# Attention in a four-layer graph network: destination rows gathered into their own tiles and added on GpSimd

## The chip, the cores and the metric

The kernel runs on one core of one Trainium2 chip. Times are microseconds (us) on the device for one execution; a change is judged by the median of several runs. The names of the engines are those of the profile: PE is TensorE's matmul, PEld its weight load, DVE is VectorE, ACT is ScalarE, POOL is GpSimd, SP is SyncE, which here only issues DMAs.

## The reference, cut to what matters

Four graph layers run one after another over 6,250 nodes with 160 features (64 scalars and 32 vectors of 3) and 100,000 edges sorted by destination. Each adds its result to x. The change lies in layer 2, an attention layer. What its edges begin with is, for every edge, the sum of two rows that were computed per node:

```
s_src, v_src = node rows mapped by Ws_src, Wv_src      # table[2]
s_dst, v_dst = node rows mapped by Ws_dst, Wv_dst      # table[3]
message[e]   = row_src[src[e]] + row_dst[dst[e]]       # 160 floats for each edge
```

The sum is weighted by a map of the edge attributes, multiplied with the edge's 4 numbers (scalar and vector products), mapped, gated and multiplied once more; that gives the edge's scores and its value row. A softmax over the edges of each destination and a weighted sum follow in later passes.

## The kernel before

Edges are padded and cut into NG = 196 groups of 512: TG = 4 tiles of P = 128 edges, one edge to a partition. `attention_pass` is the stage that the change touches. It holds one program for each engine, every one a loop over the groups (`steps`, with an unroll of U = 4), joined by semaphores alone. `at_least` is a wait; `gate` is several waits, the first on a semaphore that has long been settled.

- SP's step i loads `ends[s]` for group i (the 4 columns of source indices and the 4 of destination indices, s = i mod 4), once `joined[s]` says that the slot's old indices have been used. Behind that, in the same queue, come the edge attributes of group i-2, the scores of group i-4 and the message rows of group i-7.
- POOL's step i waits for the indices of group i and for `made1` of group i-4 (the DVE has finished its first part on the group that held the tile `g[s]`; K1 = 13 operations), and issues four gathers from table[2] (L1114), one for each 128 x 160 tile of `g[s]`. Then it waits until group i-1's four gathers have landed (`fetched`) and issues four gathers from table[3] into the same tiles with `compute_op=ALU.add` (L1121). They count `joined`.
- ACT waits for `joined` in `scale_rows` and writes `gy` (L1216), four operations for a group. Its other work takes PE's transposes and maps out of PSUM (L1226, L1252) and applies the gates (L1265, L1267).
- DVE runs, for each group, `first` (group i: reads `g`, waits for `joined`), `message` (group i-3) and `second` (group i-1). All of them are tensor_tensor operations recorded at L1304, 28 for a group. Those on `att_vy`, `att_p` and `att_dot`, the product with `att_gate` and the two sums that end `second` take both inputs from SBUF; the others have one in PSUM.
- PE transposes the features, and maps them with the value, attention and gate weights: 90 matmuls for a group.

POOL can be three groups ahead of the DVE at most, since there are FETCH = 4 slots of `g`. Nothing else runs on POOL in this stage.

Of the kernel before, what the change touches and what calls it, by code (L numbers as in the profile page):

```python
# [22 lines left out]
P = 128  # L23
# [21 lines left out]
def build(nc, A, out):  # L45
# [86 lines left out]
    with whole:  # L132
# [825 lines left out]
        def attention_pass():  # L958
# [12 lines left out]
            with ExitStack() as ctx:  # L971
# [15 lines left out]
                ea = pair("ea", [2 * QUARTER, 2 * P])  # L987
                y_all = sums_T[:, 0:NG * TG * YC]
                g = pair("g", [P, TG, FEAT], n=FETCH)
                gy = pair("gy", [P, TG, FEAT])  # L990
                at = NG * TG * YC

# [23 lines left out]
                ea_loaded = [sem(ctx, f"att_ea_loaded{s}") for s in range(2)]  # L1016
                y_loaded = sem(ctx, "att_y_loaded")
                fetched = [sem(ctx, f"att_fetched{s}") for s in range(FETCH)]
                joined = [sem(ctx, f"att_joined{s}") for s in range(FETCH)]
                scaled = sem(ctx, "att_scaled")  # L1020
                y0_done = sem(ctx, "att_y0_done")
# [19 lines left out]
                with nc.Block() as block:  # L1041

                    @block.sync
                    def _(sp):
# [31 lines left out]
                        def step(i, s, r):  # L1076

                            if live(i, NG):
                                at_least(sp, joined[s], 16 * TG * r)
                                sp.dma_start(ends[s][:, 0:TG], A["src_groups"][ds(i * P, P), :]).then_inc(ends_loaded[s], 16)  # L1080
                                sp.dma_start(ends[s][:, TG:2 * TG], A["dst_groups"][ds(i * P, P), :]).then_inc(ends_loaded[s], 16)
                            k = i - 2
# [23 lines left out]
                    @block.gpsimd  # L1106
                    def _(pool):
                        def step(i, s, r):
                            if live(i, NG):
                                gate(pool, (w_loaded, 16 * N_LOAD),  # L1110
                                     (ends_loaded[s], 32 * (r + 1)),
                                     (made1, (i - 3) * K1))
                                for t in range(TG):
                                    pool.indirect_dma_start(g[s][:, t, :], None, table[2],  # L1114
                                                            bass.IndirectOffsetOnAxis(ends[s][:, t:t + 1], 0)).then_inc(fetched[s], 16)
                            if live(i - 1, NG):
                                s1, r1 = back(s, r, 1, U)
                                gate(pool, (w_loaded, 16 * N_LOAD),
                                     (fetched[s1], 16 * TG * (r1 + 1)))
                                for t in range(TG):  # L1120
                                    pool.indirect_dma_start(g[s1][:, t, :], None, table[3],  # L1121
                                                            bass.IndirectOffsetOnAxis(ends[s1][:, TG + t:TG + t + 1], 0),
                                                            compute_op=ALU.add).then_inc(joined[s1], 16)

                        steps(pool, NG, 1, step, warm=8, unroll=U)

# [83 lines left out]
                    def _(act):  # L1210
                        def scale_rows(i, s, r):
                            gate(act, (w_made, 9),
                                 (made1, (i - 1) * K1),
                                 (joined[s], 16 * TG * (r + 1)))
                            for t in range(TG):
                                ins = nc.scalar.activation(gy[s % 2][:, t, :], g[s][:, t, :], ACT.Copy, scale=y0_of(i, t))  # L1216
                            ins.then_inc(scaled, 1)
# [60 lines left out]
                    def _(dve):  # L1278
# [34 lines left out]
                        def first(i, s, r):  # L1313
# [3 lines left out]
                            sca0, vec0 = gy[s % 2][:, :, 0:SC], gy[s % 2][:, :, SC:FEAT].rearrange("p t (c u) -> p t c u", c=XYZ)  # L1317
                            at_least(dve, made1, k)
                            at_least(dve, made2, (i - 1) * K2)
                            at_least(dve, joined[s], 16 * TG * (r + 1))  # L1320
                            tt(vy[:, :, :, :], vec, xyz(yy, 1, 4, VC), ALU.mult, made1)
                            cross_parts(vec, yy, made1)
                            dve.wait_ge(made1, k + 1)
# [495 lines left out]
```

## Time and profile before

| | |
|---|---|
| median of 3 runs | 9227.61 us (9198.25 to 9258.36) |
| span of the profiled execution | 7226.5 us |
| the median less that span | 2001.1 us |
| busy in the span | PE 6569.0 us (91%), PEld 5175.8 (72%), DVE 4888.2 (68%), ACT 3087.1 (43%), POOL 4427.4 (61%) |
| POOL instructions of the attention stage | 784 gathers at L1114, 784 at L1121, from 2723.3 to 5285.2 us |
| mean granted TensorE clock | 0.872 of full speed |

The profile's own execution has no separate time; its span runs from the first to the last instruction. What lies around the span is taken as the median less the span, and as the same for both kernels. The attention stage lies in the 16th to the 30th of the 40 slices.

### The profile page before, as it was taken

Reading aid. Unit: us, or ns where it says so; the run is one execution under the profiler, and the core shown is the slowest. Engines: PE = TensorE matmul, PEld = TensorE weight load, DVE = VectorE, ACT = ScalarE, POOL = GpSimd, SP = SyncE. Lnnn points to the kernel's source line nnn. Section 1 sums busy time; section 2 is a strip of 40 time slices with the busy share of each in tenths; the row PEclk is TensorE's granted clock in tenths of the full one; section 3 lists DMA queues with packets and bytes.
Section 4 is the critical chain, followed back from the end, with each engine's and each line's share of the span. In section 5 each row is a group of like instructions: output and inputs, shape, how many; then the busy total and the mean of one; then the engine's idle time right before and its main releaser. Section 6 shows DMA issues by size and latency. Waiting matters only on the chain. (4 is left out here: it accounts for less than half of the span.)

```text
span 7226.5 us, 182541 instructions
## 1 busy us (share of the span) xinstructions
PE 6569.0 (91%) x51671; PEld 5175.8 (72%) x51671; DVE 4888.2 (68%) x14416; ACT 3087.1 (43%) x8581; POOL 4427.4 (61%) x3934
## 2 busy tenths in 40 slices
PE   6999999799999857999999999999947879999998
PEld 3777778576666736878878777787836744777777
DVE  4666665476666545777777777777657975666665
ACT  2444443333333344666666666666530012333332
POOL 1777773277777216888877887878720011777772
PEclk9999997599999756889898888989778955999996
DMA  1222221222222213444444444444426701222221
GB/s 61 68 68 68 68 68 34 58 68 68 69 69 68 44 60 61 83 82 83 82 81 80 82 81 81 82 80 83 78 52 174 200 5 36 69 69 69 69 69 44
DMA packets 730807, 526.10 MB, mean 73 GB/s; under 512 B 244683, under 2 KB 677819, under 8 KB 730083
## 3 DMA queue, kind: packets, MB, share of 16 engines
q0 software_dynamic: 263424, 321.38, 22.1%
q1 hardware_dynamic: 467300, 203.73, 11.0%
q8 instruction: 39, 0.64, 0.0%
q14 instruction: 44, 0.36, 0.0%
HBM read 429.13 MB, written 95.55 MB: 73 GB/s over the span
## 5 line engine op out<-in xcount | busy, mean ns | idle before, releaser
L606 POOL DMA_INDIRECT l_edge_g<-node_table,l_edge_idx x2352 | 2281.7, 970 | 1124.3 <-issue 702.9
L649 PEld LDWEIGHTS l_edge_win_ps<-l_edge_hot,l_edge_prod 128*32 128x32 f32 (+2 forms) x23520 | 1515.3, 128 | 247.7 <-issue 170.4
L649 PE MATMUL l_edge_win_ps<-l_edge_hot,l_edge_prod 128*32 128x40 f32 (+2 forms) x23520 | 1620.9, 227 | 4.3 <-DVE sums_T L732 4.3
L1121 POOL DMA_INDIRECT att_g<-node_table,att_ends x784 | 1250.4, 1595 | 238.9 <-issue 238.6
L672 ACT ACTIVATE l_edge_gy<-l_edge_g,y 128x160 f32<-128x160 f32 x2352 | 811.7, 416 | 791.9 <-DMA l_edge_g<-node_table,l_edge_idx 789.3
L1114 POOL DMA_INDIRECT att_g<-node_table,att_ends x784 | 792.8, 1011 | 415.2 <-issue 281.3
L636 PE MATMUL l_edge_w_ps<-l_edge_wo,l_edge_h 128*128 128x384 f32 (+1 forms) x3136 | 907.1, 423 | 0.2 <-ACT l_edge_h L664 0.2
L664 ACT ACTIVATE l_edge_h<-l_edge_h_ps 128x256 f32<-128x256 f32 (+1 forms) x784 | 337.8, 431 | 1126.3 <-PE l_edge_h_ps L624 1076.6
L1141 PE MATMUL att_turn<-ident,sums_T 128*128 128x128 f32 (+1 forms) x4704 | 775.0, 309 | 30.1 <-ACT sums_T L1226 23.7
L636 PEld LDWEIGHTS l_edge_w_ps<-l_edge_wo,l_edge_h 128*128 128x128 f32 (+1 forms) x3136 | 536.8, 191 | 336.1 <-issue 171.7
L1226 ACT ACTIVATE sums_T<-att_turn 128x512 f32<-128x512 f32 (+1 forms) x1176 | 665.3, 591 | 216.7 <-PE att_turn L1141 211.8
L1141 PEld LDWEIGHTS att_turn<-ident,sums_T 128*128 128x128 f32 (+1 forms) x4704 | 572.6, 154 | 205.1 <-issue 119.0
L624 PE MATMUL l_edge_h_ps<-l_edge_ea,l_edge_wi 16*128 16x256 f32 (+1 forms) x1176 | 494.6, 500 | 81.2 <-ACT l_edge_h L664 27.7
L701 DVE TENSOR_TENSOR l_edge_vy<-l_edge_g,y 128x384 f32<-128x384 f32 x588 | 325.9, 554 | 255.5 <-DMA l_edge_g<-node_table,l_edge_idx 254.1
L708 DVE TENSOR_TENSOR l_edge_prod<-l_edge_w_ps,l_edge_g 128x256 f32<-128x256 f32 x588 | 247.9, 422 | 312.7 <-PE l_edge_w_ps L636 312.5
L1216 ACT ACTIVATE att_gy<-att_g,y 128x160 f32<-128x160 f32 x784 | 270.3, 416 | 272.2 <-DMA att_g<-node_table,att_ends 271.7
L703 DVE TENSOR_TENSOR l_edge_hot<-l_edge_hot,y 128x480 f32<-128x480 f32 x588 | 383.2, 652 | 0.0
L1198 PEld LDWEIGHTS att_o<-att_w_o1v,sums_T 128*128 128x128 f32 x1568 | 290.2, 218 | 108.4 <-issue 90.9
L697 DVE TENSOR_TENSOR l_edge_hot<-iota_win,dst_rel 128x160 f32<-128x160 f32 x588 | 192.4, 327 | 253.0 <-PE l_edge_win_ps L649 231.8
L1304 DVE TENSOR_TENSOR att_vec<-att_o,sums_T 128x384 f32<-128x384 f32 x196 | 109.3, 558 | 363.8 <-ACT att_gate L1267 357.3
L1181 PE MATMUL att_o<-att_w_o2s,sums_T 96*128 96x64 f32 x1568 | 334.7, 298 | 10.6 <-ACT sums_T L1226 1.5
L1199 PE MATMUL att_o<-att_w_o1v,sums_T 128*128 128x64 f32 x1568 | 341.3, 304 | 0.0
(232 smaller groups left out, 11533.8 us busy)
## 6 DMA issues: line engine op xcount, KB each, us to landing
l_messages<-att_rows SPq DMA_DIRECT2D x196, 320.0 KB
sum_msg<-l_messages SPq DMA_DIRECT2D x196, 320.0 KB, 3.6
l_edge_g<-node_table,l_edge_idx POOLq DMA_INDIRECT x2352
att_g<-node_table,att_ends POOLq DMA_INDIRECT x1568
node_table<-l_rows SPq DMA_DIRECT2D x245, 80.0 KB, 1.6
att_ea<-in_edge_attr_T SPq DMA_DIRECT2D x196, 64.0 KB
l_scores<-att_score SPq DMA_DIRECT2D x784, 2.0 KB
l_edge_idx<-in_src_groups SPq DMA_DIRECT2D x588, 2.0 KB, 1.7
```

What stands on the lines that cost most here:

```text
L606: pool.indirect_dma_start(g[s][:, t, :], None, rows_of, bass.IndirectOffsetOnAxis(idx[s][:, t:t + 1], 0)).then_inc(fetched[s], 16)
L624: nc.tensor.matmul(h_ps[0][0:HALVES * hid, 0:HC], wi[:, :], ea[s0][:, :]).then_inc(hidden[0], 1)
L636: ins = nc.tensor.matmul(w_ps[s2][:, n * HALVES:(n + 1) * HALVES, 0:wn], h[last][s2][:, n * P:(n + 1) * P], wo[:, :])
L649: ins = nc.tensor.matmul(at, q[:, t, lo:lo + width], to[:, t, kinds, :], start=t == 0, stop=t == TG - 1)
L664: nc.scalar.activation(h[n][s1][:, :], h_ps[n][0:HALVES * hid, 0:HC], act_fn, scale=scales[n]).then_inc(active[n], 1)
L672: ins = nc.scalar.activation(gy[sk % 2][:, t, :], g[sk][:, t, :], ACT.Copy, scale=y4[:, ds((k * TG + t) * 4, 1)])
L703: nc.vector.tensor_tensor(to[:, :, 1:1 + XYZ, :], to[:, :, 0, :].unsqueeze(2).to_broadcast([P, TG, XYZ, EDGE_WIN]), xyz.to_broadcast([P, T ...
L1114: pool.indirect_dma_start(g[s][:, t, :], None, table[2], bass.IndirectOffsetOnAxis(ends[s][:, t:t + 1], 0)).then_inc(fetched[s], 16)
L1121: pool.indirect_dma_start(g[s1][:, t, :], None, table[3], bass.IndirectOffsetOnAxis(ends[s1][:, TG + t:TG + t + 1], 0), compute_op=ALU.add ...
L1141: ins = nc.tensor.transpose(turn[bank][0:width, t * P:(t + 1) * P], f[:, t, at:at + width], ident[:, :])
L1199: ins = nc.tensor.matmul(o1[:, t, PV + VC:O1W], feat_T[0][:, 2, e], w_o1v[1][:, :])
L1226: nc.scalar.activation(feat_T[n][0:width, part, :], turn[bank][0:width, :], ACT.Copy).then_inc(count, 1)
```

## The change

The destination rows get tiles of their own, `g_dst[s]`, of the same size as `g[s]` (4 x 128 x 160 floats, four slots, 10,240 more bytes for each partition), and semaphores of their own, `fetched_dst[s]`. POOL's step i now issues eight plain gathers for group i. Then it waits for both sets of group i-1 and adds them in one GpSimd tensor_tensor of 128 x 640 floats. `joined` counts 1 for a group, from that add, where it counted 16 for each of four DMAs; the three waits on it (SP, ACT, DVE) are rewritten to match.

```
+                g_dst = pair("g_dst", [P, TG, FEAT], n=FETCH)
...
+                fetched_dst = [sem(ctx, f"att_fetched_dst{s}") for s in range(FETCH)]
...
                             if live(i, NG):
-                                at_least(sp, joined[s], 16 * TG * r)
+                                at_least(sp, joined[s], r)
...
                                 for t in range(TG):
                                     pool.indirect_dma_start(g[s][:, t, :], None, table[2],
                                                             bass.IndirectOffsetOnAxis(ends[s][:, t:t + 1], 0)).then_inc(fetched[s], 16)
+                                for t in range(TG):
+                                    pool.indirect_dma_start(g_dst[s][:, t, :], None, table[3],
+                                                            bass.IndirectOffsetOnAxis(ends[s][:, TG + t:TG + t + 1], 0)).then_inc(fetched_dst[s], 16)
                             if live(i - 1, NG):
                                 s1, r1 = back(s, r, 1, U)
                                 gate(pool, (w_loaded, 16 * N_LOAD),
-                                     (fetched[s1], 16 * TG * (r1 + 1)))
-                                for t in range(TG):
-                                    pool.indirect_dma_start(g[s1][:, t, :], None, table[3],
-                                                            bass.IndirectOffsetOnAxis(ends[s1][:, TG + t:TG + t + 1], 0),
-                                                            compute_op=ALU.add).then_inc(joined[s1], 16)
+                                     (fetched[s1], 16 * TG * (r1 + 1)),
+                                     (fetched_dst[s1], 16 * TG * (r1 + 1)))
+                                nc.gpsimd.tensor_tensor(g[s1][:, :, :], g[s1][:, :, :], g_dst[s1][:, :, :], ALU.add).then_inc(joined[s1], 1)
...
-                                 (joined[s], 16 * TG * (r + 1)))
+                                 (joined[s], r + 1))
...
-                            at_least(dve, joined[s], 16 * TG * (r + 1))
+                            at_least(dve, joined[s], r + 1)
```

## Rows read from the trace of the kernel before

**Rows 1.** The page's 40 slices of the span, in tenths.

```profile
PE   6999999799999857999999999999947879999998
...
POOL 1777773277777216888877887878720011777772
PEclk9999997599999756889898888989778955999996
```

**Rows 2.** Busy time in one stretch of the attention stage; (x) counts instructions.

```profile
2850.00:5250.00 2400.00, 2284.18 (x16554) 1905.90 (x16552) 1792.34 (x5151) 1521.05 (x4232) 1920.08 (x1474) 0.87 0.43 81
```

**Rows 3.** POOL's groups of instructions, 2850 to 5250: busy us, mean ns | idle before.

```profile
L1121 POOL DMA_INDIRECT att_g<-node_table,att_ends x738 | 1177.2, 1595 | 224.9 <-issue 224.9
L1114 POOL DMA_INDIRECT att_g<-node_table,att_ends x736 | 744.7, 1012 | 255.3 <-issue 255.3
```

**Rows 4.** POOL in order of time: start, us, instruction [idle before].

```profile
3997.09 1.76 POOL L1121 DMA_INDIRECT att_g<-node_table,att_ends  x1 [0.31 <-issue]
3999.15 1.02 POOL L1114 DMA_INDIRECT att_g<-node_table,att_ends  x1 [0.30 <-issue]
...
4011.71 1.01 POOL L1114 DMA_INDIRECT att_g<-node_table,att_ends  x1 [0.30 <-issue]
...
4478.17 1.04 POOL L1114 DMA_INDIRECT att_g<-node_table,att_ends  x1 [4.30 <-issue]
...
4492.23 1.41 POOL L1114 DMA_INDIRECT att_g<-node_table,att_ends  x1 [1.80 <-issue]
```

**Rows 5.** Who waited for whom, 2850 to 5250: us, times, longest.

```profile
ACT att_gy L1216 <- DMA att_g<-node_table,att_ends: 217.9, 85, 4.0
...
DVE att_vy L1304 <- DMA att_g<-node_table,att_ends: 185.3, 87, 3.3
...
PE att_turn L1195 <- ACT sums_T L1226: 81.6, 68, 2.1
```

**Rows 6.** The DVE in order of time, around one arrival of rows.

```profile
4001.27 0.56 DVE L1304 TENSOR_TENSOR att_vy<-att_g,sums_T 128x384 f32<-128x384 f32 x1 [1.77 <-DMA att_g<-node_table,att_ends]
```

**Rows 7.** Stretches of 10 us: PE, PEld, DVE, ACT, POOL busy, PEclk, DMA.

```profile
3980.00:3990.00 10.00, 8.37 (x74) 6.95 (x73) 6.32 (x19) 5.38 (x17) 8.12 (x6) 1.00 0.52 90
4200.00:4210.00 10.00, 10.00 (x48) 8.09 (x46) 2.10 (x6) 4.64 (x14) 7.87 (x8) 0.50 0.31 52
...
4250.00:4260.00 10.00, 9.76 (x83) 8.02 (x82) 8.82 (x27) 7.40 (x21) 8.08 (x6) 1.00 0.41 71
```

**Rows 8.** The DVE in order of time over one group, while rows lay ready.

```profile
4244.73 0.56 DVE L1304 TENSOR_TENSOR att_vec<-att_o,sums_T 128x384 f32<-128x384 f32 x1 [1.08 <-ACT att_gate L1267]
...
4245.91 0.56 DVE L1304 TENSOR_TENSOR att_vec<-att_vec,att_gate 128x384 f32<-128x384 f32 x1
...
4249.30 0.56 DVE L1304 TENSOR_TENSOR att_vy<-att_g,sums_T 128x384 f32<-128x384 f32 x1 [0.16 <-DVE sums_T L1304]
...
4250.88 0.28 DVE L1304 TENSOR_TENSOR att_dot<-att_vy 128x128 f32<-128x128 f32 x1
...
4255.81 0.56 DVE L1304 TENSOR_TENSOR att_vec<-att_o,sums_T 128x384 f32<-128x384 f32 x1 [1.00 <-ACT att_gate L1267]
```

**Rows 9.** POOL's groups of the whole span, shapes kept apart.

```profile
L182 POOL IOTA iota_i<- 128x64 int32 x1 | 0.2, 178 | 0.4 <-ACTq L168 0.4
```

**Rows 10.** POOL in order of time, in the node pass ahead of attention.

```profile
2572.97 16.68 POOL L330 TENSOR_TENSOR x<-x,sums_T 128x7840 f32<-128x7840 f32 x1 [25.50 <-ACT sums_T L318]
```

**Rows 11.** The DVE in order of time, in the same stretch.

```profile
2575.50 0.26 DVE L293 BATCH_NORM_STATS2 l_stat<-sums_T  x1
2575.79 13.96 DVE L270 TENSOR_TENSOR l_stat_part<-l_stat 128x49 f32<-128x49 f32 x1
2589.78 0.24 DVE L271 TENSOR_TENSOR l_stat_part<-l_stat 128x49 f32<-128x49 f32 x1
```

**Rows 12.** The DVE's groups with both inputs in SBUF, 2850 to 5250: first and last of 12.

```profile
L1304 DVE TENSOR_TENSOR att_p<-att_g,sums_T 128x256 f32<-128x256 f32 x368 | 154.1, 419 | 0.0
...
L1304 DVE TENSOR_TENSOR att_dot<-att_dot,att_vy 128x128 f32<-128x128 f32 x184 | 52.2, 284 | 0.0
```

## The prediction

> **What bounds the kernel now.** First the page's slices [rows 1]. The attention stage is the 16th to the 30th slice. In all but its first and last PE stands at 9 tenths and POOL at 7 or 8, with the granted clock at 7 to 9 tenths. Elsewhere POOL does other work that the change doesn't touch, so all of the effect lies in these 2,562 us.
>
> Next the windows and the groups by line, in a stretch without start or end [rows 2, 3]. 738 accumulating gathers are 184.5 groups, so a group takes 2400 / 184.5 = 13.01 us. POOL's share of it: 4 x 1.012 for the plain gathers, 4 x 1.595 for the accumulating ones, together 10.43 us. Ahead of each instruction POOL is idle for 0.30 us even when nothing holds it, as its timeline shows [rows 4]; the mean ahead of the accumulating ones is 224.9 / 738 = 0.305 us. With 8 x 0.305 = 2.44 us a group costs POOL 12.87 us. Only 0.14 us of the 13.01 is left. So POOL, counted as 80% busy, has hardly a free moment: it is either generating descriptors or in the fixed gap. What is left lies in a few places like the 4.30 and 1.80 us of [rows 4]; over the whole stage there are twelve such gaps (six pairs), 46 us in all.
>
> Then the waits: who feels POOL? ACT and DVE wait for the rows in about half of the groups, 217.9 and 185.3 us [rows 5]. PE hardly waits, though: 81.6 us on ACT. To see why, compare stretches of 10 us [rows 7]. With rows in hand and at full clock PE issues 83 matmuls in 10 us and is 98% busy; a group has 90 (16554 / 184), so it wants 10.8 us, and the DVE's timeline of one such group gives 4255.81 - 4244.73 = 11.1 us [rows 8]. That is faster than POOL's 12.87, so the rows run out and PE falls to 84% (3980 to 3990). Behind that the granted clock falls to 0.5, and PE does 48 matmuls in 10 us (a group in 19 us) while being 100% busy; POOL gets ahead by one to three groups, the clock comes back, and the stock is eaten again. Over the stretch the clock was 0.87. So POOL sets the pace of the mean, and PE's slow spells are mostly paid from time in which it would have waited for POOL. It is close, however: 11.1 / 0.87 = 12.8 us is what the other engines could do at this clock.
>
> **The change part by part.** *Gathers.* Four accumulating gathers go (1.595 us each), four plain ones come. The plain ones beside the same work took 1.012 us [rows 3]: 4 x 0.583 = 2.33 us less for a group. That it is the accumulation that costs the difference is taken from the two groups of rows, which differ in nothing else but the table and the index column.
>
> *The add.* One new instruction, 128 x 640 floats. The nearest row is POOL's own tensor_tensor on 128 x 7840 floats, 16.68 us, 2.13 ns per element of a partition [rows 10]; 640 of them are 1.36 us. A fixed part can't be told from one size; POOL's shortest iota took 0.18 us for 64 elements [rows 9], so I add 0.1 us. Then the gap of 0.305. The lower bound is 1.36 + 0.30 = 1.67 us.
>
> The upper bound comes from the DVE. While POOL added its 128 x 7840 elements, DVE statistics with one input went on, 0.26 us each, but the first DVE operation with two inputs from SBUF, 128 x 49 elements, took 13.96 us and ended 0.1 us after POOL's; the next one of the same size took 0.24 us [rows 10, 11]. So the two engines exclude each other for whole instructions when both read like this. In attention the DVE spends 1208 us of 2400 in such operations (twelve groups, [rows 12]), 50% of the time or 6.6 us for a group. An add that comes at a random moment finds one running every second time and waits half of its 0.3 to 0.56 us: 0.1 us in the mean. I take this because POOL should get in between two of them; the other end is that it gets in only when a run of them ends, which is the slower rival below. The trace has no row of a POOL add that comes second.
>
> The Trainium skill speaks against the change here: "SBUF — State Buffer", section "Who interferes with whom", says that a DVE instruction with two SBUF inputs and a GpSimd instruction that reads SBUF share one read interface, the later one blocking until the first ends. By that rule the trace agrees (13.96 us). By it the DVE would lose up to one add, 1.4 us, in a group as well, which the first sum below leaves out.
>
> *Sum on POOL.* 8 x 1.012 + 8 x 0.305 + 1.36 + 0.1 + 0.1 + 0.305 = 12.40 us for a group against 12.87: 0.47 us less, times 196 = 92 us.
>
> *Waits.* The add's gate now also names `fetched_dst` of group i-1. These gathers were issued before group i's eight, 10 us earlier; the last accumulating gather before a start of the DVE ended at 3998.85 and the DVE began at 4001.27, so a landing takes some 2.4 us [rows 4, 6]. The gate costs nothing. Behind it on POOL stand the next group's gathers. `joined` now comes from the add and without the 2.4 us of landing, which shifts the DVE and ACT but no rate. On SP the wait for `joined` stands ahead of the index loads; it asks for a group that was added over two groups ago, and is early. The stock is still three groups at most. Sixteen gathers and one add now lie ahead of the first rows (16 x 1.25 + 1.7 = 21.7 us) where eight plain and four accumulating ones and a landing did (10 + 7.4 + 2.4 = 19.8): +2 us once. At the end there is a stock, so nothing.
>
> *The DVE's loss.* When the rows are short, the DVE is idle before each add ends (it waited 1.77 us in [rows 6]), so the exclusion costs nothing there. When there is a stock, the DVE has 1.0 us of idle in its group of 11.1 [rows 8]; an add of 1.4 us inside its chain makes it 11.1 to 11.5 us, still under 12.4. I put it at nothing in the forecast. Its cover is the time that POOL keeps the others waiting; where that is gone, it costs up to 0.4 us for a group.
>
> *Sum.* 92 - 2 = 90 us less; the 46 us of held gaps stay. The profiled execution: 7226.5 - 90 = 7136.5 us of span, with 2001.1 around it 9137.6, say 9138.
>
> **The rivals.** *The clock holds the others (gain lost).* The change takes from the waits of PE 0.47 us for a group, but PE's slow spells were paid from these. If the clock stays at 0.87 and the DVE's loss counts, the others need 11.1 / 0.87 = 12.8 to 11.5 / 0.87 = 13.2 us for a group against 13.01: from 41 us less to 37 more, 9187 to 9265, middle 9225. For it: the granted clock was 0.87 in the mean of the stretch [rows 2], and the other engines are already this near. Against: the fall of the clock followed a stretch with PE at 84%, and stretches at 98% kept it; with POOL at 12.4, PE would be at 11.1 / 12.4 = 90%, and stay full for longer.
>
> *The add waits for a whole run of the DVE (slower).* The DVE's operations follow one another within 0.1 us, and from 4245.91 to 4251.16 nearly all have two SBUF inputs, a run of 5.25 us in 11.1 [rows 8]. If POOL gets in only at its end, a random arrival waits 5.25^2 / (2 x 11.1) = 1.24 us in the mean, in place of 0.1: 12.40 + 1.14 = 13.54 us, plus 0.14 as now, 0.67 us more than 13.01, 131 us: 9359. It turns the sign where the mean wait passes 0.1 + 0.47 = 0.57 us.
>
> *The clock rises.* If PE at 90% keeps its clock, the held gaps go (46 us), and with an add of bare 1.36 us the sum is 0.67 x 196 + 46 - 2 = 175 us less: 9052.
>
> *It does not do what it says.* If what costs 1.6 us is the second table or index column and not the accumulation, the gathers stay as they are and the add comes on top: 1.87 us x 196 = 366 us more, 9594. Against it: both index columns lie in one tile, and both tables have rows of the same length.
>
> **How the numbers follow.** About 1% (92 us) is what a measurement of this kernel tells from no change; the runs shown spread over 60 us. Chances: forecast 0.50 (its own range 9100 to 9180, the ends being the add's bare cost, 0.67 us for a group, and half of the sum), held by the clock 0.30, slower by runs 0.10, clock rises 0.07, other cause 0.03. Faster by over 1% (under 9135) is somewhat under half of the forecast, the risen clock, and a little of the second: 0.37. Slower by over 1% (over 9320) is the run rival, the last one and a few strays of the second: 0.14. The rest, 0.49, is within 1%. The range leaves out the last one and the run rival, and half of the risen clock: 9070 to 9280.
>
> **What would show it.** In the profile after: 1568 gathers at about 1.0 us; 196 POOL adds, with mean near 1.5 us if right, 2.5 if the run rival is; POOL's group at 12.4 us; some DVE operations of 0.3 to 0.6 us stretched to about 1.5 to 2; ACT and DVE still waiting for the rows, now released by POOL; the clock at 0.87 to 0.9. If POOL shows many gaps over 1 us and few waits for rows are left, the others bind and the second case is true. The prediction is wrong as a whole if plain gathers back to back take longer than 1.01 us, if the add costs over 2 us, or if the DVE's loss lowers the clock.

## The result and the profile after: 4.8% slower

The changed kernel takes 9665.81 us (median of 4 runs, 9649.78 to 9693.4), the kernel before 9231.56 in the same comparison. The ratio is 1.0481, with an interval of 1.0441 to 1.0522: 434 us slower, where some 90 us faster was forecast.

Both kernels show two levels of time, without anything changed in the code. Kernels timed together, called a job below, all lie on one level. The comparison above lies on the upper one. The profile of before that stands ahead of the prediction is an execution on the lower one: 7226.5 us of span. I had put the other 2001.1 us around the span. The profiled execution of the changed kernel has a time of its own, 9650.05 us, and its span is 9648.2: only 1.9 us lie around it. The kernel before takes 9.2 to 9.4 ms on the upper level and 7.2 ms on the lower, and a ratio is always taken within one job.

The page of the changed kernel on the upper level, its span and its 40 slices (in tenths; the rows of before are [rows 1]), then its groups of L606, L649 and of POOL's attention lines:

```profile
span 9648.2 us, 182737 instructions
...
PE   6888888788888858888888889888884888998998
...
POOL 2555553255555225554445444554440003555552
PEclk9888887688888756666666666666666956777776
...
L606 POOL DMA_INDIRECT l_edge_g<-node_table,l_edge_idx x2352 | 2321.8, 987 | 2420.2 <-DVE l_edge_prod L716 1262.3
L649 PE MATMUL l_edge_win_ps<-l_edge_hot,l_edge_prod 128*32 128x40 f32 (+2 forms) x23520 | 2033.2, 246 | 578.0 <-issue 544.6
...
L1116 POOL DMA_INDIRECT att_g<-node_table,att_ends x784 | 761.9, 972 | 1682.7 <-issue 1548.5
...
L1119 POOL DMA_INDIRECT att_g_dst<-node_table,att_ends x784 | 742.5, 947 | 238.8 <-issue 238.8
```

POOL, which stood at 7 or 8 tenths through attention in [rows 1], stands at 4 or 5. The granted clock stands at 6 tenths in every slice of attention but the first. POOL is idle for 1682.7 us ahead of L1116: it is the one that waits. And L649, the edge passes' window matmuls, which the change doesn't touch, have 544.6 us of idle time "issue" ahead of them; in the profile of before that group had 4.3 us of idle time in all. So the two profiles can't be set side by side. The kernel before has to be profiled on the same level.

### The profile page after: what moved, and what is told of

It is laid out like the page before. It is cut to its first block and busy times, and to the rows that moved or that the text cites. A ratio compares the mean times of both kernels' runs of the same rounds, so it can differ in the third digit from the quotient of the medians.

```text
span 9648.2 us, 182737 instructions
## 1 busy us (share of the span) xinstructions
PE 8083.7 (84%) x51671; PEld 6259.3 (65%) x51671; DVE 4877.3 (51%) x14416; ACT 3083.1 (32%) x8581; POOL 4231.8 (44%) x4130
## 5 line engine op out<-in xcount | busy, mean ns | idle before, releaser
L606 POOL DMA_INDIRECT l_edge_g<-node_table,l_edge_idx x2352 | 2321.8, 987 | 2420.2 <-DVE l_edge_prod L716 1262.3
L649 PE MATMUL l_edge_win_ps<-l_edge_hot,l_edge_prod 128*32 128x40 f32 (+2 forms) x23520 | 2033.2, 246 | 578.0 <-issue 544.6
L649 PEld LDWEIGHTS l_edge_win_ps<-l_edge_hot,l_edge_prod 128*32 128x32 f32 (+2 forms) x23520 | 1841.9, 145 | 971.9 <-issue 837.6
L1116 POOL DMA_INDIRECT att_g<-node_table,att_ends x784 | 761.9, 972 | 1682.7 <-issue 1548.5
L1144 PE MATMUL att_turn<-ident,sums_T 128*128 128x128 f32 (+1 forms) x4704 | 1035.6, 387 | 317.7 <-ACT att_score L1273 222.7
L636 PE MATMUL l_edge_w_ps<-l_edge_wo,l_edge_h 128*128 128x384 f32 (+1 forms) x3136 | 1168.0, 516 | 12.5 <-issue 12.3
L1144 PEld LDWEIGHTS att_turn<-ident,sums_T 128*128 128x128 f32 (+1 forms) x4704 | 787.9, 196 | 547.5 <-ACT att_score L1273 250.9
L636 PEld LDWEIGHTS l_edge_w_ps<-l_edge_wo,l_edge_h 128*128 128x128 f32 (+1 forms) x3136 | 681.6, 238 | 473.2 <-issue 351.7
L1119 POOL DMA_INDIRECT att_g_dst<-node_table,att_ends x784 | 742.5, 947 | 238.8 <-issue 238.8
L1201 PE MATMUL att_o<-att_w_o1v,sums_T 128*128 128x64 f32 x1568 | 379.1, 333 | 37.7 <-issue 36.1
L1185 PE MATMUL att_o<-att_w_o2v,sums_T 128*128 128x64 f32 x1568 | 397.4, 346 | 0.0
L1186 PE MATMUL att_o<-att_w_o2v,sums_T 128*128 128x64 f32 x1568 | 394.6, 344 | 0.0
L1202 PE MATMUL att_o<-att_w_o1v,sums_T 128*128 128x64 f32 x1568 | 389.9, 340 | 0.0
```

The lines of the kernel that those rows point to most:

```text
L606: pool.indirect_dma_start(g[s][:, t, :], None, rows_of, bass.IndirectOffsetOnAxis(idx[s][:, t:t + 1], 0)).then_inc(fetched[s], 16)
L636: ins = nc.tensor.matmul(w_ps[s2][:, n * HALVES:(n + 1) * HALVES, 0:wn], h[last][s2][:, n * P:(n + 1) * P], wo[:, :])
L649: ins = nc.tensor.matmul(at, q[:, t, lo:lo + width], to[:, t, kinds, :], start=t == 0, stop=t == TG - 1)
L1116: pool.indirect_dma_start(g[s][:, t, :], None, table[2], bass.IndirectOffsetOnAxis(ends[s][:, t:t + 1], 0)).then_inc(fetched[s], 16)
L1119: pool.indirect_dma_start(g_dst[s][:, t, :], None, table[3], bass.IndirectOffsetOnAxis(ends[s][:, TG + t:TG + t + 1], 0)).then_inc(fetched ...
L1144: ins = nc.tensor.transpose(turn[bank][0:width, t * P:(t + 1) * P], f[:, t, at:at + width], ident[:, :])
```

## The experiments

The stages can be told apart by the first and last instruction of tiles that only they use. In the tables "attention us" runs from the start of the stage's first source gather to the start of its last, in the profiled execution, and "clock" is the mean granted TensorE clock over the whole span of that execution.

### A job on the upper level: is it the add?

Four kernels ran together. `before_again` is the kernel before, unchanged. `gathers_no_add` is the changed kernel without the add: destination rows are fetched into their own tiles and left out of the result, and a memset of one column counts `joined`. The other two are the kernel before with one more POOL instruction for a group, on tiles that nobody else uses; their results are the reference's. The cuts below leave out the setting up of tiles and semaphores.

```
gathers_no_add
-  nc.gpsimd.tensor_tensor(g[s1]..., g[s1]..., g_dst[s1]..., ALU.add).then_inc(joined[s1], 1)
+  at_least(pool, joined[s2], r2 + 1)
+  nc.gpsimd.memset(mark[:, :], 0.0).then_inc(joined[s1], 1)
before_plus_pool_tt
+  nc.gpsimd.tensor_tensor(extra[1][:, :], extra[0][:, :], extra[2][:, :], ALU.add).then_inc(extra_done, 1)
before_plus_pool_memset
+  nc.gpsimd.memset(extra[:, :], 0.0).then_inc(extra_done, 1)        # 128 x 1720
```

> The kernel before, unchanged, profiled once more. The profile shown has a span of 7226.5 us at a mean granted clock of 0.872, while the runs are 9230 us; the profile of the changed kernel has a span of 9648.2 us in a run of 9650 us, at 0.728. Theory A (the profiled execution of before was a quicker one than those that were timed, and TensorE at a low clock bounds the kernel in the timed ones): this profile has a span near 9228 us, a clock near 0.75, and in attention about 16.2 us for a group with GpSimd waiting several us in each. Theory B (2001 us lie outside the span): the span is again near 7226 us, clock 0.87, and GpSimd 12.9 us busy of 13.0 in a group.

> The changed kernel with its eight plain gathers, but the GpSimd add replaced by a memset of one column that counts joined; the destination rows are fetched and left out of the result. Theory 1 (the add costs, by its exclusion of the VectorE and the late rows): back to 9230 us, within 60. Theory 2 (the plain gathers issued in a bunch of eight cost, by their DMAs or by the moment at which the rows come): stays at 9600 to 9700 us and the add is innocent.

> The kernel before with one more GpSimd tensor_tensor of 128x640 on scratch tiles behind each group's accumulating gathers; nobody waits for it. It reads SBUF as the add does, but nothing depends on it. Theory 1a (what costs is the exclusion between GpSimd's and VectorE's two-input operations): about 9600 to 9700 us as the changed kernel. Theory 1b (what costs is that ScalarE and VectorE get the rows later, behind the add): 9230 us. Theory 2 (the gathers): 9230 us too.

> The kernel before with a GpSimd memset of 128x1720 on scratch (about 1.45 us at the 0.84 ns per element of the memsets in the trace) behind each group's accumulating gathers. It takes GpSimd as long as the add and only writes. Theory 1a: 9230 us within 60, since a memset doesn't read and holds no two-input operation of the VectorE. Rival (GpSimd's own time counts, or any operation of it slows the others): 9350 us or more.

| kernel | median us | ratio to before, interval | attention us | clock |
|---|---|---|---|---|
| kernel before in this job | 9413.86 | | | |
| before_again | 9426.79 | 1.0001 (0.9978 to 1.0025) | 3274 | 0.746 |
| gathers_no_add | 9851.99 | 1.0455 (1.0414 to 1.0496) | 3703 | 0.713 |
| before_plus_pool_tt | 9421.41 | 0.999 (0.9957 to 1.0022) | 3327 | 0.737 |
| before_plus_pool_memset | 9419.92 | 1.0003 (0.9977 to 1.003) | 3294 | 0.739 |

The add is not the cause: without it the loss is 1.0455, nearly all of the 1.0481. Nor is a busier GpSimd, nor the exclusion of VectorE, though it is there. In before_plus_pool_tt the extra instruction is recorded with 2127 ns, of which some 0.6 us lie beside the accumulating gather ahead of it (the last section shows the rows), and the DVE is 1979.25 us busy in the window 3800 to 6800 where it is 1732.74 in before_again, at nearly the same count of instructions. That costs nothing that can be measured.

Windows of the same 3000 us (columns: PE, PEld, DVE, ACT and POOL busy, PEclk, DMA share, GB/s), of before_again:

```profile
3800.00:6800.00 3000.00, 2715.11 (x15904) 2282.94 (x15902) 1732.74 (x4949) 1492.82 (x4068) 1805.77 (x1414) 0.71 0.32 63
```

of the changed kernel on this level:

```profile
3800.00:6800.00 3000.00, 2598.48 (x14550) 2150.06 (x14548) 1590.79 (x4525) 1356.17 (x3720) 1492.09 (x1457) 0.66 0.22 57
```

and of gathers_no_add:

```profile
3800.00:6800.00 3000.00, 2623.51 (x14088) 2170.56 (x14089) 1534.68 (x4385) 1310.94 (x3608) 1212.46 (x1407) 0.64 0.21 55
```

With 90 matmuls for a group these are 176.7, 161.7 and 156.5 groups, 16.98, 18.55 and 19.17 us each. PE is busy for 2715.11 / 176.7 = 15.4 us of a group, then 16.1 and 16.8, with the clock at 0.71, 0.66 and 0.64; its idle part is 1.6, 2.5 and 2.4 us. Only the first and the third come from one job: the changed kernel was timed in another one, in which before took 9231.56 us, 182 less than here, so that its 18.55 us can't be set against 16.98. From before_again to gathers_no_add a group takes 2.19 us more, 1.4 of slower matmuls and 0.8 of idle time. Times 196 that is 429 us, the whole of the stage's 3703 - 3274. Which of the two came first, the lower clock or the idle time, the rows don't show. The last groups of the stage, after the gathers have ended, take 10.9 to 11.0 us in all three.

Nobody waits for rows. POOL's groups and the longest waits of before_again in that window (us, times, longest):

```profile
L1121 POOL DMA_INDIRECT att_g<-node_table,att_ends x708 | 1112.6, 1571 | 215.7 <-issue 215.7
L1114 POOL DMA_INDIRECT att_g<-node_table,att_ends x706 | 694.5, 984 | 978.8 <-issue 978.8
```

```profile
DVE att_vec L1304 <- ACT att_gate L1267: 887.0, 145, 7.9
ACT att_rows L1245 <- PE att_o L1183: 376.6, 153, 3.6
ACT sums_T L1226 <- PE att_turn L1141: 319.7, 588, 2.1
```

POOL is idle for 978.8 / 176.7 = 5.5 us of every group ahead of its four source gathers, 4.3 of them more than the four fixed gaps, where it had nothing to spare in [rows 3]. No wait of ACT or the DVE for `att_g` is in that window, where [rows 5] has two. In the edge passes, which have plain gathers in both kernels, PE shows gaps inside a row of matmuls that wait for nothing that the profile shows. Its timeline in before_again (start, us, instruction, idle before):

```profile
528.63 2.16 PE L649 MATMUL l_edge_win_ps<-l_edge_hot,l_edge_prod 128*96 128x40 f32 x24
531.04 0.20 PE L649 MATMUL l_edge_win_ps<-l_edge_hot,l_edge_prod 128*32 128x40 f32 x1 [0.24 <-issue]
531.78 0.23 PE L649 MATMUL l_edge_win_ps<-l_edge_hot,l_edge_prod 128*32 128x40 f32 x2 [0.55 <-issue]
533.95 0.20 PE L649 MATMUL l_edge_win_ps<-l_edge_hot,l_edge_prod 128*32 128x40 f32 x1 [1.93 <-issue]
```

From 300 to 1100 us PE does 5156 matmuls there at a clock of 0.86, where the profile of before on the lower level has 7515 at 1.00. What is longer on the upper level is the stages that gather and use PE together: 1487 us for the first edge pass against 1022, 3274 for attention against 2547. The sums by destination (317 against 316 us) and the last 100 us are not.

### A job meant for the same question: the lower level

Next came kernels to split the gathers. `before_plain_second` is the kernel before with `compute_op` taken off L1121, so the destination rows overwrite the source rows and the result lacks the source rows. `source_rows_only` has four gathers for a group and no add, so it lacks the destination rows. `after_pool_filled` is the changed kernel with a second GpSimd add, of `g_dst` to itself into a spare tile, behind the first. `after_interleaved` is the changed kernel with the gathers in the old order (destination rows of group i-1 behind the source rows of group i), the add coming at group i-2.

```
before_plain_second
-                               bass.IndirectOffsetOnAxis(...), compute_op=ALU.add).then_inc(joined[s1], 16)
+                               bass.IndirectOffsetOnAxis(...)).then_inc(joined[s1], 16)
source_rows_only
-  for t in range(TG): pool.indirect_dma_start(g_dst[s]..., table[3], ...)
-  nc.gpsimd.tensor_tensor(g[s1]..., g[s1]..., g_dst[s1]..., ALU.add).then_inc(joined[s1], 1)
+  nc.gpsimd.memset(mark[:, :], 0.0).then_inc(joined[s1], 1)
after_pool_filled
+  nc.gpsimd.tensor_tensor(extra[:, :, :], g_dst[s1]..., g_dst[s1]..., ALU.add).then_inc(extra_done, 1)
after_interleaved
-  for t in range(TG): pool.indirect_dma_start(g_dst[s]..., table[3], ...)     # group i
+  for t in range(TG): pool.indirect_dma_start(g_dst[s1]..., table[3], ...)    # group i-1
-  nc.gpsimd.tensor_tensor(g[s1]..., g_dst[s1]..., ALU.add)                    # group i-1
+  nc.gpsimd.tensor_tensor(g[s2]..., g_dst[s2]..., ALU.add)                    # group i-2
```

> The kernel before with one word less: the second four gathers of each group have no compute_op, so they overwrite the source rows in g with the destination rows in place of adding. Order, waits and semaphores are those of before. The result lacks the source rows. Theory P or Q (what costs is that the second gathers no longer accumulate; they are cheaper for GpSimd, 0.95 against 1.57 us, and for the DMA engines): 1.04 to 1.06 times before, attention 3600 to 3750 us from first to last gather, clock in it 0.64 to 0.67. Theory R (what costs is that all eight gathers are issued in one bunch, or that the rows come at another moment): 1.00, 3270 us, 0.71.

> The changed kernel without its destination gathers and without the add: four gathers for a group, and a memset of one column that counts joined. The result lacks the destination rows. GpSimd's work is 5.2 us for a group. Theory P (the less GpSimd holds the others, the lower the clock): as slow as the kernel with eight gathers and no add or slower, 1.045 to 1.07. A theory by which gathers as such cost (their DMAs or descriptors disturb the others): faster than that kernel, 1.00 or below.

> The changed kernel with one more GpSimd tensor_tensor of 128x640 (g_dst plus itself, into a scratch tile) behind each group's add; nobody waits for it but GpSimd's own next gathers. GpSimd's work for a group grows from 11.7 us to 13.3 to 13.8, above the 12.9 of before. Theory P (GpSimd's time for a group sets how fast the others may run when their clock is full, and a slower one keeps the clock up): back towards before, ratio 1.00 to 1.02. Theory Q (it is the accumulating DMA itself, not GpSimd's time): stays at 1.045 or more. Theory R: stays.

> The changed kernel with its gathers in the order of before: step i issues the source gathers of group i, then, when these of group i-1 have landed, the destination gathers of group i-1 into g_dst, and then adds group i-2 (a group later than in the changed kernel). GpSimd's work is the same 11.7 us. Theory R (the bunch of eight): back to 1.00 to 1.01. Theory P or Q: 1.04 to 1.05.

| kernel | median us | ratio to before, interval | attention us | clock |
|---|---|---|---|---|
| kernel before in this job | 7205.47 | | 2547, profile of before | 0.872 |
| before_plain_second | 6844.82 | 0.9502 (0.9485 to 0.952) | 2168 | 0.913 |
| source_rows_only | 6827.09 | 0.9473 (0.9458 to 0.9489) | 2153 | 0.915 |
| after_pool_filled | 7422.7 | 1.0298 (1.0281 to 1.0315) | 2770 | 0.846 |
| after_interleaved | 7520.23 | 1.044 by all four executions, 1.034 by the faster two | 2775 | 0.848 |

This job was on the lower level, so it can't say what makes the gathers dear on the upper one, and half of the expectations lost their ground. It says what the prediction was about: on the level of the profile that I had read, taking the accumulation off is worth 5.0%, and then even half of the gathers less gains at most 0.3% more.

Window 2850 to 5000 of before_plain_second, with POOL's groups there:

```profile
2850.00:5000.00 2150.00, 2052.65 (x16993) 1721.38 (x16992) 1848.61 (x5282) 1555.88 (x4340) 1501.05 (x1482) 0.99 0.35 94
```

```profile
L1121 POOL DMA_INDIRECT att_g<-node_table,att_ends x744 | 768.7, 1033 | 226.8 <-issue 226.8
L1114 POOL DMA_INDIRECT att_g<-node_table,att_ends x738 | 733.1, 993 | 324.7 <-issue 324.7
```

The groups now come every 11.1 us (2168 / 196; the window reaches 0.1 ms past the last gather), and the clock, 0.87 in nearly the same stretch of before [rows 2], is 0.99 and doesn't fall once the stage is under way. POOL needs 4 x 1.033 + 4 x 0.993 + 8 x 0.305 = 10.5 us for a group. That is under 11.1, and the trace has no wait for rows in this window; the slow spells of some 20 us for a group are gone with them. source_rows_only, whose POOL has half of the gathers, is no faster than 11.0 us for a group: the other engines set the pace of both. The window of after_pool_filled is the opposite:

```profile
2850.00:5000.00 2150.00, 2022.05 (x13526) 1710.36 (x13524) 1859.71 (x4212) 1252.25 (x3454) 1619.94 (x1508) 0.80 0.27 74
```

PE does a fifth fewer matmuls at a clock of 0.80. The extra instruction took 1258 ns; the mean of a group went to 14.3 us, of which POOL's instructions and gaps make 13.2. In its profiled execution after_interleaved looks much the same, 14.2 us for a group at a clock of 0.81, though POOL has no more to do than in the changed kernel. Its waits, 2850 to 5000:

```profile
POOL att_g L1116 <- issue: 517.9, 606, 8.9
...
ACT att_gy L1223 <- POOL att_g L1130: 247.1, 87, 4.6
...
DVE att_vy L1311 <- POOL att_g L1130: 125.6, 49, 3.9
```

ACT and the DVE wait for the add, which comes a group later, while POOL has 2.2 us idle in a group beyond its fixed gaps. The next job gives the changed kernel 0.9754 on this level. after_interleaved differs from it only in the order of the gathers and in adding a group later, and is some 6% slower (1.034 against 0.9754). The prediction had put a shift of the rows at nothing ("shifts the DVE and ACT but no rate"); a shift the other way, by a whole group, is no small thing here. Order and delay were not told apart.

### The changed kernel on the lower level, and another place for the add

```
add_on_vector
-  POOL, group i-1:  nc.gpsimd.tensor_tensor(g[s1]..., g[s1]..., g_dst[s1]..., ALU.add).then_inc(joined[s1], 1)
+  DVE, group i+1, between message(i - 3) and second(i - 1):
+                    at_least(dve, fetched[s], 16 * TG * (r + 1))
+                    at_least(dve, fetched_dst[s], 16 * TG * (r + 1))
+                    nc.vector.tensor_tensor(g[s]..., g[s]..., g_dst[s]..., ALU.add).then_inc(joined[s], 1)
```

`changed_again` is the changed kernel, `plain_second_b` and `source_rows_b` are the two cut ones again, all without a new edit. `add_on_vector` computes all of the reference.

> The changed kernel, unchanged, beside the three below. Runs so far fall into two kinds by the chip: the kernel before takes 7205 us on one and 9414 us on another. On one of 7205 us: theory L (GpSimd's add excludes the VectorE, the delay reaches TensorE, and its clock falls) expects 1.03 to 1.05, as for the two kernels with the add that ran there, attention near 14.2 us for a group. On one of 9414 us: 1.045 as before. A ratio under 0.99 on the first kind would show that the bunch without another GpSimd operation is good there.

> The kernel before without compute_op in its second gathers, as in before_plain_second (0.950 where before takes 7205 us, 11.1 us for a group at full clock). On a chip where before takes 9414 us: theory S (there TensorE is held by something that gathers add to, and GpSimd's cheaper gathers come in denser bursts) expects 1.02 to 1.05; theory T (there the cost of the changed kernel comes from issuing eight in one bunch) expects 0.98 to 1.00.

> Four gathers for a group and no add, as in source_rows_only (0.947 where before takes 7205 us). Where before takes 9414 us: if gathers as such hold TensorE back there (through the DMA engines or GpSimd's descriptors), half of them gives 0.95 or less. If, other way round, GpSimd's slow gathers protect the clock there, it is 1.045 or more.

> The changed kernel with its add of 128x640 on the VectorE, a group ahead, between message and second; GpSimd only gathers, eight plain ones in a bunch. VectorE's work grows from 9.7 to about 10.6 us for a group. Theory L on a chip of 7205 us: no exclusion is left, the VectorE has 1.0 us of idle in a group of 11.1, so 0.95 to 0.97 and a correct result. If any 0.9 us more on the VectorE's chain is enough to make the clock fall, 1.00 to 1.05. On a chip of 9414 us: as the kernel without the add, 1.04 to 1.05.

| kernel | median us | ratio to before (7196.02 us), interval | attention us | clock |
|---|---|---|---|---|
| changed_again | 7046.52 | 0.9754 (0.9679 to 0.9828) | 2351 | 0.899 |
| plain_second_b | 6839.17 | 0.9502 (0.9479 to 0.9525) | 2177 | 0.911 |
| source_rows_b | 6831.18 | 0.9491 (0.9468 to 0.9514) | 2153 | 0.914 |
| add_on_vector | 6854.25 | 0.9527 (0.9505 to 0.9549) | 2174 | 0.912 |

Here is the turn of the case: on the lower level the same change makes the kernel 2.5% faster. Its four executions took 6973 to 7087 us, where those of the other three in this job stay within 32 us each. The plain gathers bring 5.0%, and the add on GpSimd gives half of that back. On the DVE the same add gives back nothing that can be told: 0.9527 against 0.9502 here, 0.9496 against 0.9513 in the next job. Windows and POOL's groups of changed_again, 2850 to 5000:

```profile
2850.00:5000.00 2150.00, 2033.98 (x16012) 1709.64 (x16012) 2014.36 (x4977) 1467.15 (x4091) 1685.31 (x1605) 0.95 0.34 88
```

```profile
L1119 POOL DMA_INDIRECT att_g_dst<-node_table,att_ends x712 | 718.7, 1009 | 217.0 <-issue 217.0
L1116 POOL DMA_INDIRECT att_g<-node_table,att_ends x714 | 690.5, 967 | 244.7 <-issue 208.4 <-DVE sums_T L1307 32.9 <-DMA att_g_dst<-node_table,att_ends 2.9
L1126 POOL TENSOR_TENSOR att_g<-att_g,att_g_dst 128x640 f32<-128x640 f32 x179 | 277.5, 1550 | 3.0
```

POOL and the DVE in order of time around two of its adds:

```profile
3528.48 1.56 POOL L1126 TENSOR_TENSOR att_g<-att_g,att_g_dst 128x640 f32<-128x640 f32 x1
...
4016.94 1.55 POOL L1126 TENSOR_TENSOR att_g<-att_g,att_g_dst 128x640 f32<-128x640 f32 x1
```

```profile
3528.29 2.78 DVE L1307 TENSOR_TENSOR att_p<-att_g,sums_T 128x256 f32<-128x256 f32 x4
...
4016.35 2.56 DVE L1307 TENSOR_TENSOR att_vy<-att_g,sums_T 128x384 f32<-128x384 f32 x1 [0.26 <-DVE sums_T L1307]
```

Four `att_p` operations with both inputs in SBUF, two of 128 x 256 and two half as long, take 2.78 us beside the first add; two at the 419 ns of [rows 12] and two at the 297 ns that the short form takes in the mean of this stretch make 1.43. Beside the second add one `att_vy` of 0.56 us takes 2.56: it began 0.59 us before the add and ended 0.42 us after it. Over the stretch `att_p<-att_g` of 128 x 256 takes 853 ns in the mean against 419 [rows 12], up to 2359. The DVE is busy for 2014.36 / 177.9 = 11.3 us of a group of 12.1, with 90 matmuls for a group giving the count; in before_plain_second it was 1848.61 / 188.8 = 9.8. POOL is fuller still. From one add to the next it has, in 161 of the 178 groups of this window, only its fixed gaps, 2.3 us in all, and these groups take 11.75 us in the mean; in the other 17 it was held, and the mean is 12.1. POOL's add itself stays between 1537 and 1564 ns over all 196: the DVE is the one that is held. By the Trainium skill ("SBUF — State Buffer", section "Who interferes with whom") the later of the two blocks until the first ends; the trace agrees that whole instructions exclude each other, but not on which one is held. Both adds began after a DVE operation had begun, by 0.19 and 0.59 us, and neither was longer than the others; the DVE operation was. The measurement decides here. The window of add_on_vector:

```profile
2850.00:5000.00 2150.00, 2059.31 (x17027) 1727.43 (x17026) 1985.41 (x5483) 1559.00 (x4348) 1588.46 (x1481) 0.99 0.36 94
```

The DVE has one more operation for a group, of 0.82 us, and PE is not held up: 17027 matmuls at 0.99, as without any add. POOL has no add.

### Trying the upper level again

Three kernels were timed again, to settle on the upper level whether the destination gathers, the missing accumulation or the number of gathers costs the 4.6%.

> Four gathers for a group and no add, once more, for a chip where before takes 9414 us. There the stages without gathers (sum of the messages 317 us, last stage 100 us) take as long as on the chip of 7205 us, and those with gathers 1.3 to 1.45 times as long (first edge pass 1487 against 1022 us, attention 3274 against 2547), and the last groups of attention, when no gather is left, run at 10.9 us. Theory G (gathers hold TensorE back on that kind of chip) expects under 0.95 there; the theory that slow gathers protect the clock 1.045 or more. On a chip of 7205 us again 0.949.

> The kernel before without compute_op, in its own order of gathers, for a chip where before takes 9414 us. Theory G with density (what counts is how many gathers start in a time): 1.03 to 1.05 there. Theory T (the bunch of eight counts): 0.98 to 1.00 there. On a chip of 7205 us again 0.950.

> Eight plain gathers in a bunch and the add on the VectorE, for a chip where before takes 9414 us: 1.04 to 1.05 by theory G with density and by theory T. On a chip of 7205 us again 0.953.

This job too was on the lower level (before 7206.03 us): source_rows_c 6831.81 (0.9481), plain_second_c 6849.9 (0.9513), add_on_vector_c 6841.97 (0.9496). It repeats that the three lie within 0.4% of one another, and nothing else. Three jobs of one kernel each followed.

> Four gathers for a group and no add, once more, for a session where before takes 9200 to 9400 us. Theory G (gathers hold TensorE back in such a session) expects under 0.95 there; the theory that slow gathers protect the clock 1.045 or more. In a session where before takes 7200 us again 0.949.

> Eight plain gathers in a bunch and the add on the VectorE, once more, for a session where before takes 9200 to 9400 us: 1.03 to 1.05 if it behaves there as the kernel without any add (1.0455), which would make it no better version in such a session; 1.00 or below if that kernel's loss was its own. In a session where before takes 7200 us again 0.950 to 0.953.

> Four gathers for a group and no add, for a session where before takes 9240 us, as the one just before (there eight plain gathers with the add on the VectorE were 1.0475). Theory G (gathers hold TensorE back in such a session) expects under 0.95; the theory that a GpSimd with less to do lets the clock fall further expects 1.045 or more, attention 3600 us or more from first to last gather. In a session where before takes 7200 us again 0.947.

source_rows_d (6823.22, 0.9462, before 7210.81) and source_rows_e (6829.63, 0.9464, before 7209.91) were on the lower level once more. add_on_vector_d was on the upper one: 9684.72 us against 9241.88, a ratio of 1.0475 (1.041 to 1.054), with 3615 us of attention. Its window 3800 to 6800:

```profile
3800.00:6800.00 3000.00, 2643.47 (x14477) 2187.66 (x14477) 1697.38 (x4666) 1353.51 (x3699) 1260.80 (x1288) 0.65 0.22 57
```

It is the changed kernel's row but for POOL and the DVE: a clock of 0.65 and 14477 matmuls. So on the upper level three kernels with eight plain gathers into two sets of tiles, and the add on GpSimd, on the DVE or nowhere, lose 4.8, 4.75 and 4.55%. What they share is the eight plain gathers, their order (all eight of a group in a row) and the second set of tiles.

## Why the prediction was wrong

**The failed step** is the first one, the choice of the execution on which all rests: that 2001.1 us lay around the span, so that a span of 7226.5 stood for a median of 9227.61. It is 1.9 us. The timed executions had spans near 9230 us and another balance. "POOL sets the pace" (12.87 of 13.01 us) was true of the profile, and false of them: POOL was idle for 4.3 us of a group of 17.0 in before_again beyond its gaps ahead of the source gathers. With that the 92 us of saving on POOL had nothing to act on. The profile held the warning: 2 ms outside the span of a kernel of 7 ms, put down to nothing that it showed.

**The clock as the holder of the others** was the right rival in kind and too small in size. It was built on a clock that stays at 0.87, with 9265 us as its end. On the upper level the clock in the middle of attention was 0.71 in before_again and 0.64 in gathers_no_add, of the same job. That the plain gathers themselves could cost something beside TensorE was in no case of mine; the slower rival rested on the add, and the runs clear the add.

**On the lower level the steps can be checked one by one.** *Gathers:* 1.012 us was expected for the plain ones, and 1.009 and 0.967 came; before_plain_second shows with one keyword that it was the accumulation and not the table or column that cost 1.6 us, so the rival of another cause falls. *The add:* 1.36 + 0.1 + 0.1 = 1.56 us expected, 1.550 measured. The sum is right and its last part is not: no add waited for the DVE (1537 to 1564 ns), so the terms met by luck. *POOL's group:* 12.40 us expected; 4 x 1.009 + 4 x 0.967 + 8 x 0.305 + 1.55 = 11.9 measured. The gathers make 0.19 us of the difference, and the gap of 0.305 us ahead of the add, which isn't there, the rest. *Sum:* POOL's group fell from 12.87 to 11.9 us, the stage from 2547 / 196 = 13.0 us a group to 2351 / 196 = 12.0. So where POOL had nothing to spare, "POOL sets the pace" held, and 0.97 x 196 = 190 us is what the sum gives with the measured terms. The stage was 196 us shorter, and the times, which spread, differ by 7196.02 - 7046.52 = 150 us where 90 were forecast. The last rival, "the clock rises", had 175 us, but by other terms (the held gaps gone, a bare add of 1.36 us); POOL was still held in 17 groups, so its nearness is luck. The clock in the stretch did rise, from 0.88 to 0.95.

**The DVE's loss, put at nothing,** was 11.3 - 9.8 = 1.5 us of busy time for a group, near the 1.4 us that the prediction named. On this level no run shows that it cost time, since POOL alone was full in nine groups of ten. The add on GpSimd as a whole does cost time: moving it to the DVE takes the ratio from 0.9754 to 0.9527, 192 us by the medians and 163 by the ratios, or 0.8 to 1.0 us for a group. POOL's 11.75 to 11.9 us against the 11.1 of the others would make 0.65 to 0.8 of it; how much is that and how much the exclusion was not told apart. The run rival is refuted: no add came later than its bare time, so GpSimd gets in at once.

**What stays open.** Why the kernels with plain gathers show a lower TensorE clock and more idle time on the upper level than those with accumulating ones. The rows show less DMA share (0.22 against 0.32) and less of POOL beside the lower clock. gathers_no_add rules the add out as the cause of the 4.8%, and with it its exclusion; the two kernels with an extra instruction rule out a busier POOL. Whether it is the missing accumulation, the order of all eight in a row, or the number of gathers, was not told apart: before_plain_second, source_rows_only and after_interleaved never fell on that level. Open too is what puts a whole job on one level or the other. In the expectations I put it down to the chip, but the record lists chip 6 for one job on the upper level and one on the lower. All that the traces show is its signs: gaps inside rows of matmuls that wait for nothing seen, and a lower clock, in stages that gather beside TensorE, in the changed and in the unchanged kernel.

## What to carry to other kernels

Before a term is costed, check that the profile is of an execution like the timed ones: here the span and the time differed by 1.9 us when they were of the same execution, and a gap of 2 ms meant another one. Where one engine paces a stage, a saving on it counts until the next engine's pace is reached: 0.97 us less on POOL took 1.0 us off a group, 2.4 us less (before_plain_second) took only 1.9 off, since 11.1 us was what the others needed. An add that costs GpSimd 1.55 us is dear where GpSimd has nothing to spare: it cost the group 0.8 to 1.0 us more there than on the DVE, though the DVE was the busier engine before the change. So try such an add in a gap of the other engine. Don't take a later add for free either: a group later, with the gathers in the old order, went with some 6%. And judge a version at both levels, since the one that gained 4.7% at 7.2 ms (0.9527) lost as much as the change at 9.2 (1.0475).

## What the runs showed that I had not expected

The kernel before takes 7.2 ms in five jobs and 9.2 to 9.4 in three, on one core each time, and one change reads as 0.9754 or 1.0481 at either.

The accumulating gather costs POOL 1.57 to 1.60 us in the mean against 0.95 to 1.09 for a plain one, at both levels. A GpSimd tensor_tensor of 128 x 640 floats takes 1.55 us when it adds into one of its inputs behind a plain gather, and 1.26 behind another add when both inputs are one tile; whether form or place makes the difference was not told apart. The 2.13 us of before_plus_pool_tt are no price of the form. Its rows:

```profile
5004.43 1.54 POOL L1128 DMA_INDIRECT att_g<-node_table,att_ends  x1 [0.30 <-issue]
5005.41 2.12 POOL L1132 TENSOR_TENSOR att_extra<-att_extra 128x640 f32<-128x640 f32 x1
```

The instruction is recorded from 0.98 us after the start of the accumulating gather, which lasts 1.54; behind the gather's end it takes 1.56 us, as the add does. The memset of before_plus_pool_memset lies in the same way, 2128 ns in the mean, where I had expected 1.45.
